# LoRA factor transposed in pairs on two halves of the partitions, small loads on another queue, first addition ahead of the threshold network

## The reference

```python
x = x + _L0_cond_ref(x, W0, b0, coeff, mask)     # x @ W0.T + b0 + coeff[b] * (x @ (2*mask[b]-1))
x = x + _L1_cond_ref(x, weight, scale_log, codebook, lora_A, lora_B)
x = x + _L2_cond_ref(x, tok2, W2, b2, As, Bs)    # dense layer plus a rank-16 adapter per batch
x = x + _L3_cond_ref(x, A, B, tok3)              # rank-16 adapter per batch

def _L1_cond_ref(x, weight, scale_log, codebook, lora_A, lora_B):
    lora_delta = lora_B @ lora_A * (32.0 / 64)         # (1024 x 64) @ (64 x 1024)
    cb = codebook / max(abs(codebook))
    scale = exp(scale_log)                             # one per row and group of 128 columns
    normalized = (weight + lora_delta).reshape(1024, 8, 128) / scale
    thresholds = (cb[:-1] + cb[1:]) * 0.5              # 7 of them
    quantized = cb[searchsorted(thresholds, normalized)]
    return x @ (quantized * scale + lora_delta).T
```

## Time and profile before

| | |
|---|---|
| median of 3 runs | 580.99 us (580.81 to 581.22) |
| the profiled execution | 579.73 us, of which the trace spans 578.0 us |
| granted TensorE clock, mean | 0.994 |
| TensorE busy | 555.5 us, 96% of the span |
| VectorE busy | 382.5 us, 66% |
| ScalarE busy | 307.8 us, 53% |
| GpSimd busy | 127.3 us, 22% |
| chain that ended last, by engine | PE 80%, DVE 6%, DMA 4%, SyncE's queue 4%, ACT 3% |

### The profile page before, as it was taken

How to read it: one execution, slowest core, us unless ns; L and a number is a source line. 1 busy time by engine, 2 the same in 40 slices (tenths; PEclk the granted TensorE clock), 3 DMA queues, 4 the chain that set the end, 5 groups by cost and what they waited for, 6 DMA issues and landing times.

```text
span 578.0 us, 9955 instructions
## 1 busy us (share of the span) xinstructions
PE 555.5 (96%) x3508; PEld 501.8 (87%) x3508; DVE 382.5 (66%) x575; ACT 307.8 (53%) x551; POOL 127.3 (22%) x134
## 2 busy tenths in 40 slices
PE   4889999969999899999999999999999999999997
PEld 4788988858888898898899899899889989989986
DVE  5999868857863884765677557477576666846521
ACT  3677756647653763554554555355555454635510
POOL 2778658946840100000000000000000000000000
PEclk9999999989999899999999999999999999999999
DMA  7955032453229893691583295087068229404201
GB/s 221 272 56 132 19 110 73 151 169 119 74 77 247 332 210 137 146 265 46 135 236 101 77 223 172 36 185 227 24 154 245 73 94 221 157 36 146 75 18 54
DMA packets 125898, 80.10 MB, mean 139 GB/s; under 512 B 91504, under 2 KB 107888, under 8 KB 125872
## 3 DMA queue, kind: packets, MB, share of 16 engines
q1 hardware_dynamic: 125296, 78.71, 48.7%
q0 software_dynamic: 288, 1.05, 0.5%
q10 hardware_dynamic: 288, 0.01, 0.0%
HBM read 65.59 MB, written 14.16 MB: 138 GB/s over the span
## 4 chain that ended last, share of the span: by engine, by line
PE 80%; DVE 6%; DMA 4%; SPq 4%; ACT 3%; POOL 1%; issue 1%; ACTq 0%; DVEq 0%; POOLq 0%
PE bank L1319 10%; PE bank L1318 10%; PE bank L1320 10%; PE bank L1298 10%; PE bank L1300 10%; PE bank L1299 10%; PE bank L1187 4%; PE bank L1189 4%; PE bank L1188 4%; SPq L310 2%; PE bank L1091 1%; DMA mask_ring<-in_mask_Bx4096x_ik 1%; PE bank L1327 1%; PE bank L1326 1%; PE bank L1334 1%
## 5 line engine op out<-in xcount | busy, mean ns | idle before, releaser
L1298 PE MATMUL bank<-x_t_hi,m_hi 128*128 128x256 f32 x512 | 145.9, 285 | 2.9 <-DVE P_lo L895 2.1
L1299 PE MATMUL bank<-x_t_lo,m_hi 128*128 128x256 f32 x512 | 145.6, 284 | 0.0
L1300 PE MATMUL bank<-x_t_hi,m_lo 128*128 128x256 f32 x512 | 145.5, 284 | 0.0
L690 ACT CAST m_hi<-merged_ring 128x512 fp32r<-128x512 f32 x128 | 76.8, 618 | 80.9 <-PE bank L1300 52.4
L992 DVE TENSOR_TENSOR m_lo<-merged_ring,m_hi 128x512 fp32r<-128x512 f32 x128 | 84.1, 689 | 29.5 <-ACT m_hi L690 29.4
L1298 PEld LDWEIGHTS bank<-x_t_hi,m_hi 128*128 128x128 f32 x512 | 98.9, 193 | 3.8 <-DVE m_lo L992 3.5
L1318 PE MATMUL bank<-P_hi,x_t_hi 128*128 128x512 f32 x256 | 99.8, 390 | 0.0
L1319 PE MATMUL bank<-P_lo,x_t_hi 128*128 128x512 f32 x256 | 99.8, 390 | 0.0
L1320 PE MATMUL bank<-P_hi,x_t_lo 128*128 128x512 f32 x256 | 99.6, 389 | 0.0
L1299 PEld LDWEIGHTS bank<-x_t_lo,m_hi 128*128 128x128 f32 x512 | 99.0, 193 | 0.3
L1300 PEld LDWEIGHTS bank<-x_t_hi,m_lo 128*128 128x128 f32 x512 | 99.0, 193 | 0.0
(11 more groups left out here) (147 smaller groups left out, 899.4 us busy)
## 6 DMA issues: line engine op xcount, KB each, us to landing
mask_ring<-in_mask_Bx4096x_ik SPq DMA_DIRECT2D x64, 512.0 KB, 3.8
x_squares<-in_x SPq DMA_DIRECT2D x64, 128.0 KB, 3.1
out<-out_staged SPq DMA_DIRECT2D x32, 256.0 KB, 2.1
w_nat<-in_L_cond_W SPq DMA_DIRECT2D x15, 512.0 KB, 4.5
w_raw<-in_L_cond_weight SPq DMA_DIRECT2D x16, 256.0 KB, 4.5
g_batch<-g_dram SPq DMA_DIRECT2D x32, 128.0 KB, 3.9
w0t_dram<-w_out SPq DMA_DIRECT2D x14, 256.0 KB, 2.6
w_t<-w0t_dram SPq DMA_DIRECT2D x7, 512.0 KB, 7.5
```

Of the source, the lines that this page charges most:

```text
L690: nc.scalar.copy(Mh[:, n % MR], ring_f[:, k % MR, h * HALF:(h + 1) * HALF]).then_inc(s["h_set"], 1)
L1298: mm(dst, mh, xTh[:, k], start=(k == 0 and o % 2 == 0), stop=False, skip_group_check=True)
L1299: mm(dst, mh, xTl[:, k], start=False, stop=False, skip_group_check=True)
L1300: ins = mm(dst, ml, xTh[:, k], start=False, stop=(k == KT - 1), skip_group_check=True)
```

## The change

Four things change, all in the preparation.

1. **Pairs.** The factor B is loaded so that one row of `lb_nat` holds row p of the lower half (h = 0) and of the upper half (h = 1) side by side, 2 x 64 values. One 128x128 transpose then turns a block of both: h = 0 comes out on partitions 0 to 63, h = 1 on 64 to 127. Four transposes in place of eight, one copy of 128x512 on ScalarE in place of two of 64x512, and `lora_b_t` is half as wide.
2. **Deltas.** `delta(n)` reads 64 partitions of both tiles: 0 to 63 for even n, 64 to 127 for odd n. `lora_a` is therefore loaded twice, once on each set. The two memsets of padding on VectorE go.
3. **Loads.** `lora_a` comes in two parts: its first 128 columns (two small loads) ahead of the first weights, the other 896 columns (two loads) between the second and the third load of W2; `delta(2)` waits for them. `lb_nat` is two loads. The codebook and the scale are issued by ScalarE behind the tokens.
4. **Order on VectorE.** `add_delta(0)` stands right behind the reciprocal; the network and the scaled first level follow it, ahead of `add_delta(1)`.

```diff
-    lbn = at("lb_nat", [P, KT, RL], F32, lo + 28 * KB)
+    lbn = at("lb_nat", [P, HT, 2, RL], F32, lo + 28 * KB)
-    lbt = at("lora_b_t", [P, D], F32, reg_b2)
+    lbt = at("lora_b_t", [P, HALF], F32, reg_b2)
...
-            sp.dma_start(lbn[:, :, :], lora_b.rearrange("(t p) r -> p t r", p=P)).then_inc(s["lora_b_in"], 16)
-            sp.dma_start(la[0:RL, :], lora_a).then_inc(s["lora_a_in"], 16)
-            sp.dma_start(cb[:, :], row(codebook).broadcast_to([P, NCB])).then_inc(s["cb_in"], 16)
-            sp.dma_start(sc[:, :, :], scale_log.rearrange("(t p) g o -> p t (g o)", p=P)).then_inc(s["sc_in"], 16)
+            for h in range(2):
+                sp.dma_start(lbn[:, :, h, :], lora_b.rearrange("(h t p) r -> h p t r", p=P, h=2)[h]).then_inc(s["lora_b_in"], 16)
+            for h in range(2):
+                sp.dma_start(la[h * RL:(h + 1) * RL, 0:P], lora_a[:, 0:P]).then_inc(s["lora_a_in"], 16)
             for h in range(2):
                 sp.dma_start(raw[:, h], w1_cols[h, 0]).then_inc(w1_in[h], 16)
             for t in range(KT):
+                if t == 2:
+                    for h in range(2):
+                        sp.dma_start(la[h * RL:(h + 1) * RL, P:D], lora_a[:, P:D]).then_inc(s["lora_a_rest"], 16)
...
+            act.dma_start(cb[:, :], codebook.rearrange("(o n) -> o n", o=1).broadcast_to([P, NCB])).then_inc(s["cb_in"], 16)
+            act.dma_start(sc[:, :, :], scale_log.rearrange("(t p) g o -> p t (g o)", p=P)).then_inc(s["sc_in"], 16)
...
-            for h in range(2):
-                act.wait_ge(s["lbt_tr"], h + 1)
-                nc.scalar.mul(lbt[0:RL, h * 512:(h + 1) * 512], bank[5 + h][0:RL, :], L1_SCALE).then_inc(s["lbt_set"], 1)
+            act.wait_ge(s["lbt_tr"], 1)
+            nc.scalar.mul(lbt[:, :], bank[5][:, :], L1_SCALE).then_inc(s["lbt_set"], 1)
...
-            for h in range(2):
-                for t in range(HT):
-                    ins = nc.tensor.transpose(bank[5 + h][0:RL, t * P:(t + 1) * P], lbn[:, h * HT + t, :], ident[:, :])
-                ins.then_inc(s["lbt_tr"], 1)
+            for t in range(HT):
+                ins = nc.tensor.transpose(bank[5][:, t * P:(t + 1) * P], lbn[:, t].rearrange("p h r -> p (h r)"), ident[:, :])
+            ins.then_inc(s["lbt_tr"], 1)
...
+                rows = slice(h * RL, (h + 1) * RL)
                 for t in range(HT):
-                    k = h * HT + t
-
-                    ins = mm(dps(n)[:, t * P:(t + 1) * P], lbt[:, k * P:(k + 1) * P], la[:, q * P:(q + 1) * P],
+
+                    ins = mm(dps(n)[:, t * P:(t + 1) * P], lbt[rows, t * P:(t + 1) * P], la[rows, q * P:(q + 1) * P],
                              start=(t == 0), stop=True, skip_group_check=True)
```

More of the change, by code:

```diff
@@ L193, in cond_resid_chain @@
         NORM = 6
-        s = {n: sem(n) for n in """cb_in sc_in late_in lora_b_in lora_a_in w1_in0 w1_in1 a2_in b2_in a3_in b3_in w0_in w0_in2 w0_out_st0 w0_out_st1 g_stored y_stored
+        s = {n: sem(n) for n in """cb_in sc_in late_in lora_b_in lora_a_in lora_a_rest w1_in0 w1_in1 a2_in b2_in a3_in b3_in w0_in w0_in2 w0_out_st0 w0_out_st1 g_stored y_stored
             ub_in b2row_in x_in0 x_in1 g_in recip_set first_level tok_in b2c_in numbers_set rows_set ident_set ident_zero own_a own_b own_set ub_zero
@@ L200, in cond_resid_chain @@
             s_set v_set h_set m_ready m_used l0_done x1_hi x1_ready x_turned xt_hi xt_ready u_done u_hi u_ready c_ready
-            out_done out_added out_st0 out_st1 lora_pad now_set""".split()}
+            out_done out_added out_st0 out_st1 now_set""".split()}
         w2_in = [sem(f"w2_in{t}") for t in range(KT)]
@@ L920, in _, with c @@
             add_delta(0)
+            def c(i):
+                return th[:, i:i + 1]
+            step.did(nc.vector.tensor_tensor(c(1), c(1), c(3), ALU.min))
+            link(nc.vector.tensor_tensor(c(5), c(5), c(3), ALU.max))
+            step.did(nc.vector.tensor_tensor(c(0), c(0), c(1), ALU.min))
+            step.did(nc.vector.tensor_tensor(c(2), c(2), c(1), ALU.max))
+            step.did(nc.vector.tensor_tensor(c(4), c(4), c(3), ALU.max))
+            link(nc.vector.tensor_tensor(c(6), c(6), c(5), ALU.max))
+            step.did(nc.vector.tensor_tensor(c(2), c(2), c(3), ALU.min))
+            link(nc.vector.tensor_tensor(c(4), c(4), c(5), ALU.min))
+            nc.vector.tensor_scalar(cs[:, :, :], sc[:, :, :], cb[:, 0:1], None, ALU.mult).then_inc(s["first_level"], 1)
             add_delta(1)
@@ L1073, in _ @@
             pe.wait_ge(s["ident_set"], 1)
-            pe.wait_ge(s["lora_b_in"], 16)
-            for h in range(2):
-                for t in range(HT):
-                    ins = nc.tensor.transpose(bank[5 + h][0:RL, t * P:(t + 1) * P], lbn[:, h * HT + t, :], ident[:, :])
-                ins.then_inc(s["lbt_tr"], 1)
+            pe.wait_ge(s["lora_b_in"], 32)
+            for t in range(HT):
+                ins = nc.tensor.transpose(bank[5][:, t * P:(t + 1) * P], lbn[:, t].rearrange("p h r -> p (h r)"), ident[:, :])
+            ins.then_inc(s["lbt_tr"], 1)
             def delta(n):
@@ L1086, in delta @@
                 elif n == 0:
-                    pe.wait_ge(s["lbt_set"], 2)
+                    pe.wait_ge(s["lbt_set"], 1)
+                elif n == 2:
+                    pe.wait_ge(s["lora_a_rest"], 32)
+                rows = slice(h * RL, (h + 1) * RL)
                 for t in range(HT):
-                    k = h * HT + t
-                    ins = mm(dps(n)[:, t * P:(t + 1) * P], lbt[:, k * P:(k + 1) * P], la[:, q * P:(q + 1) * P],
+                    ins = mm(dps(n)[:, t * P:(t + 1) * P], lbt[rows, t * P:(t + 1) * P], la[rows, q * P:(q + 1) * P],
                              start=(t == 0), stop=True, skip_group_check=True)
@@ L1112, in w0_transpose @@
                 ins.then_inc(s["w0_tr"], 1)
-            pe.wait_ge(s["lora_pad"], 2)
-            pe.wait_ge(s["lora_a_in"], 16)
+            pe.wait_ge(s["lora_a_in"], 32)
             delta(0)
```

13 lines of the change are left out of this document (removed).

## The result

The changed kernel takes 583.92 us (median of 9 runs, 582.16 to 586.42), the kernel before, measured beside it, 580.99 (9 runs). The ratio is 1.0045, 95% interval 1.0032 to 1.0058: slower by 2.9 us by the medians and 2.6 by the ratio, where 580.0 was forecast. The measured time is outside the range (579.4 to 583.5), and on the side of the rival in which TensorE empties at each change of form (582.9).

What follows compares the result with a forecast made beforehand. Bound by VectorE's dense stretch from 13.3 us, then TensorE from 39 to 97 and 122 to 156. -0.98 at the start plus 18 x 0 gave 580.0 us for the median, range 579.4 to 583.5.

Steps and rivals of the forecast that it cites:

- the rival in which TensorE empties at each change of form: Nine deltas in TensorE's dense stretches: 18 x 0.161 = 2.90 us lost, less 0.98, 582.9 us; chance 0.26, weights' load included.
- the price s of a change of form: TensorE's cost for each switch between 64- and 128-partition matmuls: taken as 0, with 0.075, 0.161 and 0.353 us also considered.
- Deltas on 64 partitions: TensorE's narrow deltas: pace stays that of the columns, 18 changes of form are paid in full, each taken at 0.
- the one for an emptied TensorE: Upper bound per change of form: a matmul's duration, 275 ns, less its pace in a stream, 114 ns: 0.161 us.
- the count of 18: Changes of form paid in full: into and out of six deltas between 39 and 97 us, three between 122 and 156.
- the start's 0.98: VectorE's comparisons were to begin at 12.28 in place of 13.26 us: 0.98 us gained.
- Nothing in the trace has such a stop: Argument in the forecast against TensorE emptying at each change of form, which would cost 0.161 us or more each.
- Which stretches count: VectorE limits from 13.3 to 39 us; TensorE's added time is paid in full from 39 to 97 and 122 to 156.
- Transposes, copy, first deltas: Start: one copy from 6.80 to 7.39, deltas from 7.54, `delta(0)` done at 9.52; TensorE gains 0.85 us.
- Order on VectorE: Start: codebook at 7.0, first addition at 9.62, second at 11.62, comparisons at 12.28 us; almost nothing from the reorder alone.
- Loads: Start's loads hidden; the second `lora_a` copy makes W2's third tile at most 1.5 us later, covered by GpSimd's idle time: nothing.
- Everything to 97 us lies 1 us earlier: Sign that the forecast is right: the gain at the start carries through the profile up to 97 us.

Runs made afterwards that it cites:

- experiment 1: Kernel before, with all 16 deltas reading the lower 64 partitions of both tiles and nothing else changed: 583.88 us, ratio 1.0047.
- experiment 2: Changed kernel, with the deltas on 128 partitions again, lora_b_t's halves padded with zeros: 580.23 us, ratio 0.9987.
- experiment 3: Changed kernel, with the two large lora_a loads ahead of W2's sixth tile instead of the third: 583.31 us, ratio 1.0036.
- experiment 4: Changed kernel, with deltas on 128 padded partitions and the large lora_a loads ahead of W2's sixth tile: 580.25 us, ratio 0.9991.
- experiment 5: Changed kernel, with padded 128-partition deltas, later large lora_a loads, and group 2's weight issued ahead of SyncE's eight indexed loads: 577.74 us, ratio 0.9955.
- experiment 6: Kernel before, with only deltas 2, 3, 10, 11 and 12 on the lower 64 partitions: 580.56 us, ratio 0.9995.
- experiment 10: Kernel before, with group 2's weight issued ahead of SyncE's eight indexed loads and nothing else: 580.74 us, ratio 1.0001.
- experiment 7: Kernel before, with the first and third of each delta's four matmuls on the lower 64 partitions: 588.96 us, ratio 1.0149.
- experiment 9: Changed kernel, narrow deltas kept, with later large lora_a loads and group 2's weight ahead of SyncE's eight indexed loads: 580.96 us, ratio 1.0000.

## Why the prediction was wrong

The step that failed is the price s of a change of form, in "Deltas on 64 partitions": "I take 0, as the row of the same kind (a delta's pace by its columns) is the nearest, and keep both ends." It costs 0.17 us on average (0.34 a delta in the trace; 2.96 / 18 = 0.16 by the medians of experiment 1; 0.19 where there are four in a delta). The pace of columns was no row of the same kind at all: it told of steady streams, and the question was a border between two. Of the bounds, the one for an emptied TensorE, 0.161 from the earlier trace rows, was right within 0.01 to 0.03, and the count of 18 was right too: experiment 1 lost 2.96 where 18 x 0.161 is 2.90. Both numbers stood in the text with the wrong weight. With them the sum is 582.9, the second rival's; the measured 583.92 is 1.0 above it, as if nothing of the start's 0.98 had arrived (how much did is the matter of experiments 2 to 5). The Trainium skill, "TensorEngine Tiling (Array Packing)", section Tiling Modes, Key Properties, says that a change of tiling mode drains TensorE. For 64 rows against 128 the trace agrees in so far as the first load of the new form stands at 52.78, with its matmul, where that load ran 0.12 ahead before; that nothing is left in TensorE then is not shown. The rival's 0.161, a duration less the pace, fits in size; that the stop is made up in that way is not shown either. "Nothing in the trace has such a stop" was true and no evidence, as the kernel before never changed form in a dense stretch.

Step by step:

- *Which stretches count.* Right. The deltas between 97 and 122 cost nothing (experiment 6, and the wait that is shorter by 1.01 in the changed kernel).
- *Transposes, copy, first deltas.* Right in the end. The copy ran earlier than forecast (5.64), as `lb_nat` in two halves landed 1.2 us sooner; the deltas then waited for `lora_a` until 7.22, and the first addition came at 9.40 (9.62). That two misses met so near the forecast is luck.
- *Order on VectorE.* Right in kind: 0.3 alone, 1.32 with the earlier deltas (0.98 forecast). The date under it was off: "I take 7.0, where VectorE is free of `table_rows`" held the tokens' landing fixed, but they landed 1.8 us sooner, so VectorE was free at 5.14 and the codebook was in use at 6.00.
- *Loads.* "I cost it at nothing" was wrong. The cover counted was GpSimd's idle time behind W2's third tile; that tile was in use 3.5 us later (17.70, 14.16), not 1.5 at most. What was not looked at is the indexed load `b_nat`: moved forward by 1.82 us with `table_rows`, it was taken up in the rush and landed 0.7 later than before, and TensorE waits for it (2.41, before 0.92). Moving the two large loads behind gives 2.0 us back at `delta(4)` (experiment 3).
- *"Everything to 97 us lies 1 us earlier".* Wrong in a second place, that the prediction never named: an issue of SyncE at 43 us, whose date hangs on eight serial indexed loads, was just in time. Experiments 4, 5 and 10 together show it: 0.7 without, 3.2 with the weight ahead, 0 for moving the weight alone (by the medians; by the ratios 0.5, 2.6 and 0). In the changed kernel itself this wait is not reached (the addition for `delta(4)` stands at 47.94 without one), since the loads had eaten the gain first.

The account by medians: narrow deltas +2.96 (experiment 1), the rest of the change -0.7 (experiment 2), together +2.3, where +2.93 was measured. The 0.7 left over is not settled: the intervals are 0.7 to 1.0 us wide to each side. The lower clock behind 122 us is not tied down by the traces: the stretch from there to `delta(13)` took 11.3 to 11.5 us in five of the kernels (four with wide deltas and that of experiment 7) and 12.3 to 12.7 in the other seven, among them all four whose deltas are all narrow, but also two wide ones (experiments 2 and 10). The runs speak against a share in the price: the mean granted clock over all runs is 0.993 in the kernel before, in the changed one and in that of experiment 1.

## What to carry to other kernels

A border between two kinds of work is not priced by the pace of either. If the trace never shows the border, and a bound for it is worked out from overlap that is there to lose (duration less pace), that bound is a first guess; multiply it by the borders in dense stretches. Here zeros in a 128-row operand cost nothing as against the 64 rows of data alone, so halving an operand's partitions in a stream of full ones saved no time and cost two borders.

A gain at a kernel's start arrives only if every load behind it has room: list the loads between the start and the next dense stretch with their landing dates and the waits on them. A wait of zero may be one just in time. Where the gain vanishes, look for the first date that did not move: here a queue's serial issues, and two moved lines turned 0.7 us into 3.2 by the medians (0.5 into 2.6 by the ratios).

## What the runs showed of the hardware

- Going from 128-partition to 64-partition operands and back costs 0.17 to 0.19 us each time in a dense stream on this TensorE, and 0.30 at the lower pace of the start (experiment 7). Experiment 1 uses only the lower 64 partitions and pays the same, so the size alone is enough. The first weights of the new form are not loaded ahead (52.78, with their matmul; 0.12 ahead before).
- The narrow matmuls are no quicker: 272 ns median duration, 275 with 128 partitions.
- With `delta(0)` and `delta(1)` narrow TensorE keeps its slower pace of the start for longer: 421 ns for a transpose at 14.9 us (experiment 1) against 273 at 15.0 (experiment 6).
- A VectorE addition of 128x128 took 1.24 to 1.86 us in the four traces where a sum of GpSimd ran beside it, and 0.29 to 0.34 in the eight where none did.
- Two loads of 224 KB into 64 partitions each took 10.0 us beside W2's tiles, at 243 GB/s for all traffic, and 6.1 us three tiles later (experiment 5). An indexed load of GpSimd in the same rush took 9.6 us, and 7.1 before. With the two loads moved behind, the indexed one still took 8.1 to 8.2 (experiments 4, 5 and 9). Whether the halves of the partitions or the amount in flight slow them was not tried apart.
- The eight indexed loads of the fourth layer, issued by SyncE with a register load each, held its queue for 8.3 to 8.9 us in the seven traces read for it, 1.0 to 1.1 each.
